# A Cholesky and a sign elimination beside attention: the pivot row picked by a repeated unit column, in a matrix that turns by one column a step

## What is computed

```python
h = modulate(layernorm(x), shift, scale)                  # per batch
x = x + gate_msa * attention(h, W_qkv, b_qkv, W_proj, b_proj)
x = x + gate_mlp * (gelu(modulate(layernorm(x)) @ W_fc1 + b_fc1) @ W_fc2 + b_fc2)
U, _ = jnp.linalg.qr(P)                                   # P is 576 x 64
R = expm(skew(silu(cond) @ W.T + b))                      # 64 x 64 per batch
z = x @ U;  x = x + (z @ R - z) @ U.T
```

## Time and profile before

| | us |
|---|---|
| median of 3 runs (2816.80 to 2822.41) | 2819.34 |
| the profiled execution | 2816.71 |
| its span, first to last instruction | 2815.0 |
| TensorE busy / weight loads busy | 2443.0 / 2071.6 |
| VectorE, ScalarE, GpSimd busy | 1450.4, 1080.2, 930.6 |
| granted TensorE clock, mean | 0.926 of 2.4 GHz |
| attention stage, 81 to 1512 us: TensorE / VectorE / ScalarE / GpSimd busy | 1205.6 / 997.4 / 767.6 / 703.5 of 1431 |

### The profile page before, as it was taken

The page is one execution under the profiler, slowest core; times in us unless marked ns, Lnnn a source line. Parts: engine busy times, 40 slices in busy tenths (PEclk is TensorE's granted clock), DMA queues, the critical chain, the costliest instruction groups (busy, mean ns, idle before and its releaser), DMA issues. The chain is left out here.

```text
span 2815.0 us, 49871 instructions
## 1 busy us (share of the span) xinstructions
PE 2443.0 (87%) x15225; PEld 2071.6 (74%) x15225; DVE 1450.4 (52%) x2967; ACT 1080.2 (38%) x2298; POOL 930.6 (33%) x1979
## 2 busy tenths in 40 slices
PE   6687979889798797897986657999999999999998
PEld 1566757667576575675754256999999999999998
DVE  3577776767767667667763264233223323333332
ACT  2265555555555455555552120222222222222221
POOL 1054544545545454454554370111111111111110
PEclk9798989989999898998997755999999999999999
DMA  6122121221212212222111631010111011101100
GB/s 216 34 72 60 56 83 46 74 61 56 83 46 73 59 51 63 61 73 61 55 50 39 199 97 44 10 37 27 46 35 41 26 37 31 37 26 37 32 28 26
DMA packets 90996, 160.95 MB, mean 57 GB/s; under 512 B 23488, under 2 KB 34960, under 8 KB 90704
## 3 DMA queue, kind: packets, MB, share of 16 engines
q1 hardware_dynamic: 77840, 110.61, 13.8%
q0 software_dynamic: 11856, 46.60, 5.0%
q10 hardware_dynamic: 1024, 0.26, 0.0%
HBM read 80.23 MB, written 20.30 MB: 36 GB/s over the span
## 5 line engine op out<-in xcount | busy, mean ns | idle before, releaser
L1618 PE MATMUL bank<-h2T,w 128*128 128x256 f32 x4032 | 531.3, 283 | 10.4 <-issue 7.6
L1618 PEld LDWEIGHTS bank<-h2T,w 128*128 128x128 f32 x4032 | 508.2, 191 | 12.0 <-issue 8.8
L1529 DVE TENSOR_TENSOR glo<-bank,ghi 128x256 fp32r<-128x256 f32 x288 | 122.2, 424 | 714.7 <-ACT bank L1499 714.7
L1631 PE MATMUL bank<-w,ghi 128*128 128x288 f32 x2304 | 482.8, 301 | 0.4
L709 ACT ACTIVATE phi<-bank 128x512 fp32r<-128x512 f32 x512 | 303.1, 592 | 306.4 <-PE bank L1003 280.0
L1498 ACT ACTIVATE ghi<-bank,b 128x256 fp32r<-128x256 f32 x288 | 136.9, 475 | 729.1 <-PE bank L1618 729.0
L838 DVE TENSOR_TENSOR plo<-pf,phi 128x512 fp32r<-128x512 f32 x512 | 365.4, 714 | 88.2 <-ACT pf L712 82.5
L831 DVE TENSOR_REDUCE negm<-bank 128x1 f32<-128x512 f32 x512 | 349.1, 682 | 103.9 <-PE bank L975 87.9
L1631 PEld LDWEIGHTS bank<-w,ghi 128*128 128x128 f32 x2304 | 369.4, 189 | 5.7 <-DVE x2T L1539 2.1
L1631 PE MATMUL bank<-w,glo 128*128 128x288 f32 x1152 | 341.2, 296 | 0.0
L712 ACT ACTIVATE pf<-bank 128x512 f32<-128x512 f32 x512 | 303.1, 592 | 0.0
(11 more groups left out here) (217 smaller groups left out, 3560.0 us busy)
## 6 DMA issues: line engine op xcount, KB each, us to landing
xln<-x POOLq DMA_DIRECT2D x16, 1152.0 KB, 6.4
qs<-qkhi SPq DMA_DIRECT2D x192, 72.0 KB
ks<-qkhi SPq DMA_DIRECT2D x192, 72.0 KB
wst<-w_fc POOLq DMA_DIRECT2D x34, 288.0 KB, 3.1
x_d<-xln POOLq DMA_DIRECT2D x32, 288.0 KB, 2.5
xa<-x_d SPq DMA_DIRECT2D x32, 288.0 KB, 2.8
xs<-x_d SPq DMA_DIRECT2D x16, 576.0 KB, 3.8
out<-xs SPq DMA_DIRECT2D x16, 576.0 KB, 2.9
```

The lines of the kernel that those rows point to most:

```text
L1618: mm = pe.matmul(F[ft % 2][:, 0:CH], w1[0:rows, w, ft * PAR:(ft + 1) * PAR], h[0:rows, a, :], start=(i == 0), stop=(i == len(FULL_PASSES) ...
L1631: mm = pe.matmul(Y[2 * tt + half][:, 0:HALF], g[ft % 2][:, span], w2[:, ft, w, half * HALF:(half + 1) * HALF], start=(ft == 0 and i == 0), ...
```

## The change

- The pivot row is no longer masked. TensorE multiplies by one column of the identity, read 128 times over (`pick[:, h:h + 1].to_broadcast([PAR, PAR])`), with the matrix itself as moving operand. The masks, the column copies and the ones are gone. `pick_rows` copies the 16 columns that a batch needs, of the identity and of `below`, once a batch at slot 0.
- The matrix lies in two buffers of 128 partitions. A step reads one and writes the other shifted left by one column, so the pivot column is always column 0 and needs no register address. The Cholesky matrix is 128 columns wide: the identity is not stored, the finished factor is written into the column that comes free.
- TensorE waits for `row_ready`, raised when the step before has written its matrix, and for `picked`. VectorE takes 128 or 64 columns.
- The sign step has other small operations (twice, less1, shifted) and nine counted operations instead of thirteen with its mask; the Cholesky step seven instead of eight with an uncounted mask.
- `run_phases` gives TensorE and VectorE two loops (batches 1 to 3, 4 to 6), as GpSimd had. ScalarE and SyncE keep one.

```diff
-        chol = sb(every, "chol", [RANK, 3 * RANK])
-        lu = sb(every, "lu", [RANK, RANK])
+        chol = [sb(every, f"chol{i}", [PAR, 2 * RANK]) for i in range(2)]
+        lu = [chol[1][:, i * RANK:(i + 1) * RANK] for i in range(2)]
 ...
-                pool.memset(scol[:, :], 0.0).then_inc(const_ready, 1)
+                pool.memset(scol[:, :], 1.0).then_inc(const_ready, 1)
 ...
+                for i in range(2):
+                    dve.memset(chol[i][:, :], 0.0).then_inc(chol_init, 1)
+                dve.wait_ge(chol_init, 2)
                 dve.wait_ge(g_mm, 1)
-                dve.wait_ge(const_ready, 6)
-                dve.tensor_copy(chol[:, 0:RANK], PB[5][0:RANK, 0:RANK]).then_inc(chol_init, 1)
-                dve.tensor_copy(chol[:, RANK:2 * RANK], ident[0:RANK, 0:RANK]).then_inc(chol_init, 1)
-                dve.tensor_copy(chol[:, 2 * RANK:3 * RANK], ptop[:, :]).then_inc(chol_init, 1)
+                dve.tensor_copy(chol[0][0:RANK, 0:RANK], PB[5][0:RANK, 0:RANK]).then_inc(chol_init, 1)
+                dve.tensor_copy(chol[0][0:RANK, RANK:2 * RANK], ptop[:, :]).then_inc(chol_init, 1)
 ...
-        masked_row = sb(acts, "masked", [PAR, 3 * RANK])
-        masked = masked_row[0:RANK, :]
-        ones128 = sb(acts, "ones128", [PAR, PAR])
-        prow = sb(acts, "prow", [RANK, 3 * RANK])
-        small = sb(acts, "small", [RANK, 9])
-        inv, factor, minus1, sign, placed, onehot, neg, column, pivot = (
-            small[:, i:i + 1] for i in range(9))
+        prow = sb(acts, "prow", [RANK, 2 * RANK])
+        pick = sb(acts, "pick", [PAR, HEADS])
+        lower = sb(acts, "lower", [RANK, HEADS])
+        scaled = sb(acts, "scaled", [RANK, 2 * RANK])
+        small = sb(acts, "small", [RANK, 7])
+        minus1, inv, less1, twice, shifted, placed, factor = (small[:, i:i + 1] for i in range(7))
 ...
+        def run_phases(engine, slot, between=None):
+            for b in (-1, 0):
+                for n in range(SLOTS):
+                    slot(b, n, 0)
+            with engine.Fori(1, BATCH // 2) as b:
+                for n in range(SLOTS):
+                    slot(b, n, 0)
+            if between is not None:
+                between()
+            with engine.Fori(BATCH // 2, BATCH - 1) as b:
+                for n in range(SLOTS):
+                    slot(b, n, 1)
+            for b in (BATCH - 1, BATCH):
+                for n in range(SLOTS):
+                    slot(b, n, 1)
+        def pivot_matrix(phase, h):
+            return lu[h % 2] if phase else chol[h % 2]
 ...
-                CHOLESKY_OPS, LU_OPS, TURN_OPS = 8, 13, 2
-                def mask_row(k, base, matrix):
-                    pool.wait_ge(elim, base + 1)
+                CHOLESKY_OPS, TURN_OPS, SIGN_OPS = 7, 3, 9
+                def pick_rows(b, phase):
+                    pool.wait_ge(row_ready, b * HEADS + 1 + phase)
                     alone(pool)
-                    pool.tensor_copy(onehot[:, :], ident[0:RANK, bass.ds(k, 1)]).then_inc(elim, 1)
-                    pool.tensor_copy(neg[:, :], below[:, bass.ds(k, 1)]).then_inc(elim, 1)
-                    pool.tensor_copy(column[:, :], matrix[:, bass.ds(k, 1)]).then_inc(elim, 1)
+                    first = (b - phase * (BATCH // 2)) * HEADS
+                    pool.tensor_copy(pick[:, :], ident[:, bass.ds(first, HEADS)]).then_inc(picked, 1)
+                    pool.tensor_copy(lower[:, :], below[:, bass.ds(first, HEADS)]).then_inc(picked, 1)
+                def cholesky_step(b, h):
+                    base = (b * HEADS + h) * CHOLESKY_OPS + 1
+                    old, new = chol[h % 2][0:RANK, :], chol[(h + 1) % 2][0:RANK, :]
+                    pool.wait_ge(g_free, g_use(b, ("el", h)) + 3)
+                    pool.wait_ge(picked, 2 * b + 2)
+                    pool.wait_ge(elim, base)
+                    alone(pool)
+                    pool.tensor_tensor(inv[:, :], prow[:, 0:1], minus1[:, :], ALU.pow).then_inc(elim, 1)
+                    pool.tensor_tensor(placed[:, :], prow[:, 0:1], pick[0:RANK, h:h + 1], ALU.mult).then_inc(elim, 1)
+                    pool.wait_ge(elim, base + 2)
+                    alone(pool)
+                    pool.tensor_scalar(factor[:, :], old[:, 0:1], inv[:, :], lower[:, h:h + 1], ALU.mult, ALU.mult).then_inc(elim, 1)
+                    pool.tensor_tensor(dcol[:, :], dcol[:, :], placed[:, :], ALU.add).then_inc(elim, 1)
                     pool.wait_ge(elim, base + 4)
                     alone(pool)
-                    pool.tensor_scalar(masked[:, 0:matrix.shape[1]], matrix[:, :], onehot[:, :], None, ALU.mult).then_inc(row_masked, 1)
-                def cholesky_mask(k):
-                    mask_row(k, k * CHOLESKY_OPS, chol)
-                def cholesky_step(k, b, h):
-                    base = k * CHOLESKY_OPS + 3
-                    pool.wait_ge(g_free, g_use(b, ("el", h)) + 3)
-                    alone(pool)
-                    pool.tensor_tensor(dcol[:, :], dcol[:, :], masked[:, bass.ds(k, 1)], ALU.add).then_inc(elim, 1)
-                    pool.tensor_tensor(inv[:, :], prow[:, bass.ds(k, 1)], minus1[:, :], ALU.pow).then_inc(elim, 1)
-                    pool.wait_ge(elim, base + 3)
-                    alone(pool)
-                    pool.tensor_scalar(factor[:, :], column[:, :], inv[:, :], neg[:, :], ALU.mult, ALU.mult).then_inc(elim, 1)
-                    pool.wait_ge(elim, base + 4)
-                    alone(pool)
-                    pool.tensor_scalar(masked[:, :], prow[:, :], factor[:, :], None, ALU.mult).then_inc(elim, 1)
-                    pool.wait_ge(elim, base + 5)
-                    pool.tensor_tensor(chol[:, :], chol[:, :], masked[:, :], ALU.add).then_inc(elim, 1)
+                    pool.tensor_scalar(scaled[:, 1:2 * RANK], prow[:, 1:2 * RANK], factor[:, :], None, ALU.mult).then_inc(elim, 1)
+                    pool.tensor_copy(new[:, 2 * RANK - 1:2 * RANK], factor[:, :]).then_inc(elim, 1)
+                    pool.wait_ge(elim, base + 6)
+                    pool.tensor_tensor(new[:, 0:2 * RANK - 1], old[:, 1:2 * RANK], scaled[:, 1:2 * RANK], ALU.add).then_inc(elim, 1)
+                    pool.wait_ge(elim, base + 7)
+                    pool.sem_inc(row_ready, 1)
                 def turn_to_signs():
-                    base = RANK * CHOLESKY_OPS
-                    pool.wait_ge(elim, base + 1)
+                    base = RANK * CHOLESKY_OPS + 1
+                    pool.wait_ge(elim, base)
                     pool.tensor_tensor(invroot[:, :], dcol[:, :], mhalf[0:RANK, 0:1], ALU.pow).then_inc(elim, 1)
+                    pool.tensor_tensor(chol[0][0:RANK, RANK:2 * RANK], chol[0][0:RANK, RANK:2 * RANK], ident[0:RANK, 0:RANK],
+                                       ALU.add).then_inc(elim, 1)
                     pool.wait_ge(elim, base + 2)
                     alone(pool)
-                    pool.tensor_scalar(lu[:, :], chol[:, 2 * RANK:3 * RANK], invroot[:, :], None, ALU.mult).then_inc(elim, 1)
-                SIGNS = RANK * CHOLESKY_OPS + TURN_OPS
-                def sign_mask(k):
-                    mask_row(k, k * LU_OPS + SIGNS, lu)
-                def sign_step(k, b, h):
-                    base = k * LU_OPS + SIGNS + 3
-                    rows = masked[:, 0:RANK]
+                    pool.tensor_scalar(lu[0][0:RANK, :], chol[0][0:RANK, 0:RANK], invroot[:, :], None, ALU.mult).then_inc(elim, 1)
+                    pool.wait_ge(elim, base + 3)
+                    pool.sem_inc(row_ready, 1)
+                SIGNS = RANK * CHOLESKY_OPS + TURN_OPS + 1
+                def sign_step(b, h):
+                    base = ((b - BATCH // 2) * HEADS + h) * SIGN_OPS + SIGNS
+                    old, new = lu[h % 2][0:RANK, :], lu[(h + 1) % 2][0:RANK, :]
                     pool.wait_ge(g_free, g_use(b, ("el", h)) + 3)
+                    pool.wait_ge(picked, 2 * b + 2)
+                    pool.wait_ge(elim, base)
                     alone(pool)
-                    pool.tensor_copy(pivot[:, :], prow[:, bass.ds(k, 1)]).then_inc(elim, 1)
+                    pool.tensor_scalar(twice[:, :], prow[:, 0:1], 0.0, 2.0, ALU.is_ge, ALU.mult).then_inc(elim, 1)
+                    pool.tensor_scalar(less1[:, :], prow[:, 0:1], -1.0, None, ALU.add).then_inc(elim, 1)
                     pool.wait_ge(elim, base + 2)
+                    pool.tensor_tensor(shifted[:, :], less1[:, :], twice[:, :], ALU.add).then_inc(elim, 1)
+                    pool.tensor_tensor(placed[:, :], twice[:, :], pick[0:RANK, h:h + 1], ALU.mult).then_inc(elim, 1)
+                    pool.wait_ge(elim, base + 4)
+                    pool.tensor_tensor(inv[:, :], shifted[:, :], minus1[:, :], ALU.pow).then_inc(elim, 1)
+                    pool.tensor_tensor(scol[:, :], scol[:, :], placed[:, :], ALU.subtract).then_inc(elim, 1)
+                    pool.wait_ge(elim, base + 6)
                     alone(pool)
```

(58 more changed lines are left out.)

19 lines of the change are left out of this document (3 added, 16 removed).

## The result

The changed kernel takes 2756.2 us (median of 4 runs, 2754.4 to 2758.8), the kernel before 2818.7 in the same comparison: 62.5 us less, a ratio of 0.978 (95% interval 0.977 to 0.980). The forecast was 2724 with a range of 2697 to 2770. The time lies in the range, but outside the main case (2700 to 2745) and inside that of the first rival (2745 to 2800): two thirds of the 95 us came.

A forecast was written before the change was run, and what follows sets the result against it. TensorE was taken to set the pace, idling 112.8 us before the row broadcast for GpSimd's mask. Terms 67 + 17 + 10 + 1 = 95 us off 2816.7 gave 2721.7, as a median 2724, range 2697 to 2770.

The forecast's parts named there:

- main case: Whole kernel: the summed gain of 95 us arrives, time 2700 to 2745 us; chance 0.58.
- first rival: Other waits replace the gaps, VectorE pacing slots 36 to 45 or SyncE's moves late: 53 us gain, 2766; chance 0.21.
- Masks off TensorE's path: Row broadcast: gaps at h=5, 8, 12 close, h=10 shrinks; 75 us, taken as 67, bounds 35 and 75.
- third rival: GpSimd steps not shorter, h=12 gap stays: estimated 1 us at each of 16 gaps; inside the first rival's range.
- I take off a tenth: Removed broadcast gaps were also catch-up time for other engines, so 75 us is cut to 67.
- lower bound of 35: Low end for taking masks off TensorE's path: half of the gain comes back as other waits.
- The two-kinds-of-iteration argument: Sign iterations take 10.1 us more than Cholesky for the same 758 matmuls, so gaps reach the end in full.
- signs of being wrong: Unit-column loads well over 0.2 us; gaps at h=12 or h=8; new waits for `plo` or moves of k.
- Clock and narrower pair: TensorE: sign half's slow-clock time goes, 17 us (bounds 8, 25); narrower broadcast matmul saves 10 us (bounds 0, 20).
- Two loops: Attention loop's back edges: TensorE and VectorE fall through between batches 3 and 4, 1 us, bounds 0 and 3.
- The repeated column: TensorE's weight load reading one element 128 times costs nothing extra: taken as 0, a loss left open.
- fourth rival: Repeated weight load is slower on TensorE's path: at four times, 61 us slower, 2880; chance of slower 0.04.

The follow-up runs named there:

- the load in four: Changed kernel with the load of the next x cut into four DMAs, one tile and one semaphore each: 2744.2 us, ratio 0.974.
- 192 columns: Changed kernel with TensorE streaming 192 columns again in every broadcast, VectorE still taking 128 or 64: 2759.4 us, ratio 0.980.
- The two edits: Changed kernel with the step of h=9 ahead of `invert` in slot 39 and the load of x as four DMAs: 2728.2 us, ratio 0.969.
- the order alone: Kernel before, masks kept, with GpSimd making the mask of h right behind the step of h-1: 2786.8 us, ratio 0.989.
- moving the step: Changed kernel with GpSimd's step of h=9 ahead of `invert` in slot 39: alone 2740.7 us, on top of four x DMAs 2728.2 us.
- the four versions with empty instructions: Changed kernel with both edits (2728.2 us), plus 64, 128, 32 or 16 empty TensorE instructions ahead of the MLP stage: 2731.8, 2732.0, 2729.9, 2728.8 us.

## Why the prediction was right and wrong

**Masks off TensorE's path: the mechanism right, the conversion wrong.** The gaps at h=10 add up to 37.2 us over eight batches (forecast 47.8 - 12.6 = 35.2); one in the sign half, and what is left at h=12, to set beside the earlier trace rows:

```profile
896.49 0.66 PE L970 MATMUL bank<-chol,pick 128*128 128x64 f32 x2 [5.30 <-POOLq L613]
...
922.36 0.41 PE L970 MATMUL bank<-chol,pick 128*128 128x64 f32 x2 [0.98 <-POOLq L613]
```

The h=5 gaps are gone. 10.9 us stay at h=8 and h=12, where I had left 2.5 (3.5 of them in the last batch). The steps are longer than I priced them, which goes that way; that it is the whole reason isn't shown. A sign step runs from 1062.70 to 1066.31 + 0.31 = 1066.62, 3.9 us in place of 3.5; a Cholesky step from 707.24 to 710.86, 3.6 in place of 3.1, both without the last semaphore that the forecast had counted in. Of the small operations in them several stretch from 0.18 to 0.4 or 0.7 us, as the third rival had it. So 63 us of idle time went there, against 75 forecast.

The failed step is the next one, "I take off a tenth". TensorE's idle time in the stage fell by 37.8 us, not by 67: six tenths of the 63, close to my lower bound of 35. Of the 25 us that came back, 16.8 are waits for `plo`, and the load in four takes 14.7 of these away again; the rest is spread over smaller waits. I had not seen that a gap of TensorE ahead of a deadline is also time for a transfer. The load of x was costed at nothing when what stands behind the step came to hold "nobody but GpSimd"; its cover, the gap at h=8, was removed by the same edit. I had asked who waits for the load's issue, not when it lands. The two-kinds-of-iteration argument didn't show this, since both kinds had a gap at h=8. The first rival had the right victim, VectorE around slots 36 to 45, but named SyncE's moves and not the load. Two of the forecast's own signs of being wrong came: gaps left at h=8 and h=12, and new waits for `plo`. That the time lies in the range is owed to the bounds, not to the sum.

**Clock and narrower pair: 27 forecast, 32.5 measured as busy time.** The two kinds of iteration now agree within 2 us and TensorE is busy 146.7 to 148.2 us in each, as forecast; 24.3 of the 32.5 us are in the sign half. A pair of 128 columns without a gap costs 0.23 us, against 0.22 in the forecast, set beside the earlier trace rows:

```profile
591.24 0.38 PE L970 MATMUL bank<-chol,pick 128*128 128x128 f32 x2
...
591.70 0.40 PE L1011 MATMUL bank<-plo,vv 128*73 128x512 f32 x1
591.93 0.40 PE L983 MATMUL bank<-ks,qs 108*128 108x512 f32 x1
```

591.93 - 591.24 = 0.69 in place of 0.78. With 64 columns it is 0.64 in most such places, so the sign pair costs 0.18 and not the forecast's 0.22. By busy time the narrower pair is worth the 14.3 us that 192 columns put back, which leaves some 18 of the 32.5 for the clock (17 forecast). As time, 192 columns put back cost 3.2 us of the 10 forecast: a shorter pair is partly waited out. How much of the clock's share reached the end isn't shown.

**Two loops: right.** Nothing measurable on its own, where I took 1 us, and four stops on TensorE in place of five; two of them:

```profile
617.62 0.50 PE L983 MATMUL bank<-ks,qs 108*128 108x512 f32 x1 [3.61 <-issue]
...
957.40 0.79 PE L983 MATMUL bank<-ks,qs 108*128 108x512 f32 x1 [2.79 <-issue]
```

The Trainium skill (Runtime: NRT & Kernel Launch, Instruction fetch mechanics) says that a taken branch can make an engine wait until the instructions at its target are fetched. The trace agrees in the number and place of the stops, 2.8 to 3.8 us each.

**The repeated column: right.** Its weight load takes 196 ns on average where the load of ones took 204. The fourth rival is out.

**Not in the sum:** 5.9 us in the MLP stage.

In one line, by the profiled executions: 37.8 of idle time (67 forecast) and 32.5 of busy time (27), less 9.3 outside the stage (0, or 1 the other way), is 61.0 in place of 95. The two edits that pay back the load and `invert`'s place give 28 us, and end at 2728. That this is near the 2724 forecast for the change without them is chance: the forecast had kept the gap at h=10.

## What to carry to other kernels

A gap that you remove is also the cover of every transfer issued near it. For each load list when it is issued, when it lands and when its first reader comes, and subtract the gap from that slack. Removed idle time need not come off the total in full: of the 63 us removed before the broadcast, TensorE's idle time fell by six tenths, because VectorE was needed next. Before a change of the mathematics, try the order alone: half of the gain lay there.

## What the runs showed of the hardware that was not expected

- A weight load that reads one column 128 times costs no more than one of stored ones: 196 against 204 ns on average, over 256 loads each.
- Closing the gap at h=10 doesn't give back its idle time in full: with the load in four already there, moving the step took TensorE's idle time in the stage from 161.0 to 132.5 us, and its busy time rose from 1134.4 to 1143.5 for the same products. In the four versions with empty instructions, whose attention stage is the same, it is 1137.9 to 1149.4. Nearly all of the rise lies behind the broadcast of h=10 (430.6 to 442.6 us over the eight batches); what slows the products there wasn't tried.
- A stage whose text is the same can stop once more behind a taken branch, 1.1 to 1.7 us, through an edit elsewhere. The cause is open.
